# Projecting two head pairs per matmul, in a fused attention and expert layer on one core

## The chip, the cores and the metric

The kernel runs on one core of a Trainium2 chip. A core has a matrix engine (TensorE, PE in the profile; PEld are its weight loads), a vector engine (VectorE, DVE), an activation engine (ScalarE, ACT), a general engine (GpSimd, POOL) and a queue engine that starts transfers (SP). Each runs its own instructions in order, and they meet at semaphores only. TensorE writes its results to PSUM, which VectorE and ScalarE read. The metric is device time in microseconds (us): 525.79 us for the kernel before, the median of three runs (525.74 to 526.81).

## The reference

Input x is 16 rows of 256 tokens by 128 channels. The output is x plus two branches, both fed with the layer norm xn of x.

```
qkv = xn @ Wqkv + bqkv                       # 16 heads of 8
q, k = features(q), features(k)              # 8 -> 64: normalise, project with omega, clip, exp
out_t = sum_{s<=t} (q_t.k_s) v_s / max(sum_{s<=t} q_t.k_s, 1e-6)     # causal, no softmax
attention = out @ Wout + bout
logits = rms(xn) @ rms(slot_embeds)^T        # 256 tokens x 512 slots
slots = softmax(logits, tokens)^T @ rms(xn)
experts = softmax(logits, slots) @ (gelu(slots @ w1) @ w2)
```

## The kernel before, in words

One input row (256 tokens) is one turn of `row(b, ...)`; there are 16. Each engine has its own `row`, written out by hand as eight steps s = 0 to 7, one for each pair of heads. The order in it is the order of the engine's work, and every dependency is a semaphore wait (`after`, or `hold`, which waits in an instruction of its own). `bp` is the row before, `b1` the next, `b2` the one after that. So work of three rows is interleaved.

The attention of a row goes through these steps:

- `qkv_bias`, `qk_norms`, `qk_newton` (VectorE), `squares` and `qk_apply` (GpSimd) give normalised q and k of the next row. `stack_high` (ScalarE) and `stack_low` (GpSimd) write them as high and low fp16 parts into `stack`; `turn_stack` (SP queue) turns the stack round with one transposing transfer into `stack_t`.
- `project(b, p)` multiplies one pair's part of `stack_t` (96 rows) by omega, into the one PSUM bank `p_feat`: two matmuls of 256 columns, one for q and one for k. `clip` (VectorE) takes it to `arg`, `feature_exp` (ScalarE) to `feat`.
- `scores(b, p)` is eight matmuls with 64 rows and 64 columns of the array, four for each head of the pair, to the banks `p_sa` and `p_sb`. `evac_a` (VectorE, with the causal mask) and `evac_b` (ScalarE, masked after it by GpSimd's `mask_b`) take them to `s_sb`, which has four buffers.
- `context(b, a)` multiplies the scores of four heads (two pairs) by v into `p_ctx`, `ctx_copy` and `ctx_transposed` bring it to tokens by channels, `ctx_norm` divides. `attn_back`, `attn_copy`, `attention_out` are the output projection.

The experts of the same row are `logits`, `token_maxima` and `slot_maxima` (VectorE), `shift` (subtracts the maxima by matmuls, once `mx_ok` is up), the exponentials, `slot_sums`, `slots_transposed`, `hidden` in two halves, `gelu`, `processed`, `combine`. In TensorE's `row`, `project(b1, 0)` stands behind `hidden(b, nxt, 0)` at step 6, `project(b1, 1)` at the end of step 7, and `processed(bp)` before `scores(b, 0)`.

Of the kernel before, what the change touches and what calls it, by code (L numbers as in the profile page):

```python
# [16 lines left out]
PAIRS = HEADS // 2  # L17
# [44 lines left out]
def v_col(a):  # L62

    return (HD + 1) * (a % 3)
# [20 lines left out]
def build(nc, x, Wqkv, bqkv, Wout, bout, omega, nodes, weights, gamma_x, gamma_slot, slot_embeds,  # L85
          w1, w2, out):
    with ExitStack() as ctx:
# [34 lines left out]
        node_b = sb("node_b", [32, R])  # L122
        node_b2 = sb("node_b2", [32, R])
        om_scale = sb("om_scale", [32, R])
# [6 lines left out]
        omega_f = sb("omega_f", [32, PAIRS, 128])  # L131
        omega_st = sb("omega_st", [96, PAIRS, 128], F16)
# [14 lines left out]
        stack = sb("stack", [128, 2, 4, TILES, 4, 32], F16)  # L147
        stack_t = sb("stack_t", [128, 2, 2, 4, T], F16)
        vw = sb("vw", [128, 2, TILES, HEADS, 32])
        feat = sb("feat", [128, 4, 2 * T])  # L150
        arg = sb("arg", [128, 2, 2 * T])
        s_sb = sb("s_sb", [128, 4, 2, 384])
# [19 lines left out]
        p_feat = pb("p_feat", [128, 512])  # L172
        p_sa = pb("p_sa", [128, 512])
        p_sb = pb("p_sb", [128, 512])
        p_ctx = pb("p_ctx", [128, 2, T])
# [56 lines left out]
        ft_ok = sem("ft_ok")  # L232
        cl_ok = sem("cl_ok")
# [39 lines left out]
        def stacked(a):  # L273
            return stack[:, :, :, :, a, :].rearrange("p k g j d -> p j (k g) d")

        def parted():
            return qk_n[:, :, :].rearrange("p j (h d) -> p j h d", d=32)
# [5 lines left out]
        def _(sp):  # L283
# [13 lines left out]
            def turn_stack(b):  # L297
                hold(sp, sthi_ok, count(b, 1, 1))
                hold(sp, stlo_ok, count(b, 1, 1))
                hold(sp, ft_ok, count(b, 8, -8))  # L300
                sp.dma_start_transpose(stack_t[:, b[1], :, :, :].rearrange("p k g (j t) -> p (k g j) t", t=128),
                                       stack[:, :, :, :, :, :].rearrange("p k g j a d -> p (k g j a d)")
                                       ).then_inc(d_st, 16)
# [19 lines left out]
            for hl in range(4):  # L323
                for r in range(R):
                    src = omega[r].rearrange("(g q) d m -> q d g m", q=4)[hl]
                    dst = omega_f[8 * hl:8 * hl + 8, :, :].rearrange("d (g u) f -> d g u f", u=2)[
                        :, :, hl // 2, 64 * (hl % 2) + 32 * r:64 * (hl % 2) + 32 * r + 32]
                    sp.dma_start(dst, src).then_inc(d_om, 16)
# [29 lines left out]
        def _(pool):  # L358
            pool.memset(omega_f[:, :, :], 0.0).then_inc(om_zero, 1)
            pool.memset(stack[:, :, :, :, 3, :], 0.0).then_inc(st_zero, 1)  # L360
# [62 lines left out]
            def mask_b(b, p):  # L423
                hold(pool, eb_ok, count(b, 8, p + 1))
                v = s_sb[:, p % 4, 1, :].rearrange("p (a t) -> p a t", t=128)[:, 0:3:2, :]
                m = causal[:, :].rearrange("p (a t) -> p a t", t=128)[:, 0:3:2, :]
                pool.tensor_tensor(v, v, m, ALU.mult).then_inc(mb_ok, 1)  # L427
# [26 lines left out]
        def _(act):  # L454
# [26 lines left out]
            def feature_exp(b, p):  # L481
# [3 lines left out]
                nc.scalar.activation(feat[:, p % 4, :], arg[:, p % 2, :], ACT.Exp, bias=f_bias[:, 0:1]).then_inc(fe_ok, 1)  # L485

            def evac_b(b, p):
                after(act, sb_ok, count(b, 8, p + 1))
                after(act, cx_ok, count(b, 4, p // 2 - 1))
                nc.scalar.activation(s_sb[:, p % 4, 1, :], p_sb[:, 0:384], ACT.Copy).then_inc(eb_ok, 1)  # L490

            def ctx_copy(b, g):
                after(act, cx_ok, count(b, 4, 3 + g))
                after(act, ct_ok, count(b, 1, 0))
                nc.scalar.activation(ctx_sb[:, g, :], p_ctx[:, g, :], ACT.Copy).then_inc(cs_ok, 1)  # L495
# [18 lines left out]
            def gelu(b):  # L514
                for half, bank in enumerate((x01, x23)):
                    after(act, hd_ok, count(b, 2, half + 1))
                    nc.scalar.activation(hid_t[:, 2 * half:2 * half + 2, :], bank[:, :, :],  # L517
                                         ACT.Gelu).then_inc(ge_ok, 1)
# [10 lines left out]
            spread(bqkv_bc, bqkv, 3 * C).then_inc(d_rows, 16)  # L529

# [29 lines left out]
            def row(b, first, nxt, nxt2):  # L560

                b1, b2, bp = step(b, 1), step(b, 2), step(b, -1)
                for s in range(8):
                    if s == 0 and not first:
                        proc_copy(bp)
# [6 lines left out]
                    if s == 5:  # L572
                        combine_exp(b)
                    if s == 6:
                        slots_high(b)
                    if s == 7:
                        gelu(b)
                        if nxt:
                            nc.scalar.preload_act_table_set(LN_EXP)
                        ctx_copy(b, 0)  # L580
                        if nxt:
                            feature_exp(b1, 0)
                    if s == 0:
                        feature_exp(b, 1)
# [3 lines left out]
                    if s == 0:  # L588
                        if not first:
                            ctx_copy(bp, 1)  # L590
                        if nxt:
                            xt_high(b1)
                    if s == 4 and nxt:
                        stack_high(b1)
                    if s == 5 and nxt2:
                        ln_root(b2)

            run_rows(act, row)
            last_row = (B // 2 - 1, 1)
            proc_copy(last_row)  # L600
            ctx_copy(last_row, 1)
# [4 lines left out]
        def _(dve):  # L606
# [66 lines left out]
            def clip(b, p):  # L673

                after(dve, ft_ok, count(b, 8, p + 1))
                after(dve, fe_ok, count(b, 8, p - 1))
                nc.vector.tensor_scalar(arg[:, p % 2, :], p_feat[:, :], f_low[:, 0:1], f_high[:, 0:1], ALU.max,  # L677
                                        ALU.min).then_inc(cl_ok, 1)

            def evac_a(b, p):  # L680
                after(dve, sa_ok, count(b, 8, p + 1))
                after(dve, cx_ok, count(b, 4, p // 2 - 1))
                nc.vector.tensor_tensor(s_sb[:, p % 4, 0, :], p_sa[:, 0:384], causal[:, :], ALU.mult).then_inc(ea_ok, 1)  # L683

            def ctx_norm(b):
# [3 lines left out]
                for j in range(TILES):  # L689
                    last = nc.vector.tensor_scalar(  # L690
                        den[:, j, 0:12].rearrange("p (a q) -> p q a", q=QUADS),
                        t[:, 0, j, :, HD:HD + 19:9], DEN_FLOOR, None, ALU.max)
                nc.vector.tensor_scalar(den[:, :, 12:16], t[:, 1, :, :, HD], DEN_FLOOR, None,
                                        ALU.max).then_inc(dn_ok, 1)
# [4 lines left out]
                for a in range(4):  # L699
                    rows = t[:, a // 3, :, :, v_col(a):v_col(a) + HD]  # L700
# [72 lines left out]
            dve.wait_ge(d_om, 16 * 8)  # L773
            for r in range(R):
                v = omega_f[:, :, :].rearrange("p a (h r m) -> p (a h) r m", h=2, r=R)[:, :, r, :]
# [7 lines left out]
            nc.vector.tensor_copy(omega_st[0:32, :, :], omega_f[:, :, :])  # L783
            nc.vector.tensor_copy(omega_st[32:64, :, :], omega_f[:, :, :]).then_inc(om_s, 1)
            dve.wait_ge(om_s, 2)
            nc.vector.tensor_tensor(omega_st[64:96, :, :], omega_f[:, :, :], omega_st[0:32, :, :],
                                    ALU.subtract).then_inc(om_s, 1)
# [22 lines left out]
            clip(b0, 0)  # L810
            dve.wait_ge(se_h, 1)
# [8 lines left out]
            def row(b, first, nxt, nxt2):  # L820

                b1, b2, bp = step(b, 1), step(b, 2), step(b, -1)
                for s in range(8):
# [9 lines left out]
                    if s < 7:  # L833
                        clip(b, s + 1)
                    elif nxt:
                        clip(b1, 0)
                    if s == 5:
                        slots_norm(b)
                    if s == 2 and not first:
# [4 lines left out]
                    if s == 2 and not first:  # L844
                        add_attention(bp)
                    if s == 2 and nxt:
                        qk_norms(b1)
# [285 lines left out]
```

## Time and profile before

| | |
|---|---|
| Median of three runs | 525.79 us |
| Profiled execution | 526.66 us, of which the span from first to last instruction is 524.9 us |
| TensorE busy | 473.5 us, 90% |
| VectorE busy | 354.4 us, 68% |
| ScalarE busy | 319.9 us, 61% |
| GpSimd busy | 175.4 us, 33% |
| Granted TensorE clock over the span | 1.00 |

A row of input takes about 30 us on every engine, since the rows are interleaved. Busy matmuls overlap: a matmul's time in the trace holds its way through the array, and the next one starts before it ends. What a matmul costs TensorE is therefore read from start to start. The same holds, less strongly, for two operations of VectorE in a row.

### The profile page before, as it was taken

The numbers are of one execution on the slowest core, as the hardware profiler recorded it, in microseconds if no ns is written. First come the engines' busy times: TensorE is split into PE (matmuls) and PEld (weight loads), VectorE is DVE, ScalarE is ACT, GpSimd is POOL, SyncE is SP. The second block draws the span as 40 slices with busy tenths as digits, with TensorE's granted clock in tenths as the row PEclk, the third lists the DMA queues.
The fourth block names the chain that finished last, engine by engine and source line by source line (L and its number), as shares of the span: only waits on it lengthen the run. The fifth ranks groups of instructions, "written<-read, shape, count | busy, mean of one in ns | idle before, by whom it ended". The sixth has DMA issues, their size and how long they took to land.

```text
span 524.9 us, 15159 instructions
## 1 busy us (share of the span) xinstructions
PE 473.5 (90%) x5384; PEld 378.6 (72%) x5384; DVE 354.4 (68%) x905; ACT 319.9 (61%) x560; POOL 175.4 (33%) x278
## 2 busy tenths in 40 slices
PE   4049899999999999999999999999999999999996
PEld 2037686877878787787878687787768778787775
DVE  3667587585958768594966858595775859585561
ACT  3225747667573757658484766758476675847562
POOL 4314243251424334152424325141432514243220
PEclk9999999999999999999999999999999999999999
DMA  2220202020020202002020200102020110202000
GB/s 68 64 51 2 51 12 52 1 43 22 12 51 10 50 0 55 5 10 50 10 50 5 55 0 20 40 10 50 10 50 0 37 23 10 41 12 42 12 2 10
DMA packets 45362, 14.41 MB, mean 27 GB/s; under 512 B 35224, under 2 KB 45208, under 8 KB 45336
## 3 DMA queue, kind: packets, MB, share of 16 engines
q1 hardware_dynamic: 44904, 13.80, 12.6%
q8 instruction: 16, 0.26, 0.2%
q10 hardware_dynamic: 432, 0.26, 0.2%
q14 instruction: 10, 0.08, 0.0%
HBM read 3.57 MB, written 2.10 MB: 11 GB/s over the span
## 4 chain that ended last, share of the span: by engine, by line
PE 69%; DMA 14%; ACT 5%; POOL 4%; issue 4%; SPq 2%; DVE 1%; POOLq 0%; ACTq 0%; DVEq 0%
PE x L867 18%; DMA stack_t<-stack 13%; PE p_sa L903 12%; PE x L1016 11%; PE p_ctx L920 8%; PE x L1026 5%; PE p_feat L892 5%; POOL stack L421 3%; ACT stack L478 3%; PE x L945 2%; PE x L933 2%; PE x L972 2%; PE x L980 1%; PE p_sb L903 1%; ACT ctx_sb L495 1%
## 5 line engine op out<-in xcount | busy, mean ns | idle before, releaser
L427 POOL TENSOR_TENSOR s_sb<-s_sb,causal 128x256 f32<-128x256 f32 x128 | 93.5, 730 | 270.5 <-ACT s_sb L490 268.7
L677 DVE TENSOR_SCALAR arg<-p_feat,f_low,f_high 128x512 f32<-128x512 f32 x128 | 103.1, 806 | 29.8 <-PE p_feat L892 27.4
L683 DVE TENSOR_TENSOR s_sb<-p_sa,causal 128x384 f32<-128x384 f32 x128 | 70.3, 549 | 59.7 <-PE p_sa L903 59.6
L490 ACT ACTIVATE s_sb<-p_sb 128x384 f32<-128x384 f32 x128 | 62.5, 489 | 76.7 <-PE p_sb L903 76.3
L903 PE MATMUL p_sa<-feat 64*64 64x256 f32 (+3 forms) x1024 | 100.0, 312 | 7.1 <-ACT s_sb L490 3.7
L485 ACT ACTIVATE feat<-arg,f_bias 128x512 f32<-128x512 f32 x128 | 91.6, 716 | 21.1 <-DVE arg L677 21.1
L903 PEld LDWEIGHTS p_sa<-feat 64*64 64x64 f32 x1024 | 76.2, 134 | 34.6 <-issue 27.5
L903 PE MATMUL p_sb<-feat 64*64 64x256 f32 (+3 forms) x1024 | 100.0, 313 | 0.0
L903 PEld LDWEIGHTS p_sb<-feat 64*64 64x64 f32 x1024 | 76.9, 134 | 0.0
L892 PE MATMUL p_feat<-stack_t,omega_st 96*128 96x256 f16 x256 | 50.8, 280 | 23.4 <-DMA stack_t<-stack 23.0
L1016 PE MATMUL x<-w_sb,hid_t 128*128 128x128 f32 x512 | 59.8, 275 | 0.0
L1016 PEld LDWEIGHTS x<-w_sb,hid_t 128*128 128x128 f32 x512 | 58.5, 192 | 0.3
L920 PE MATMUL p_ctx<-s_sb,vw 128*32 128x256 f32 (+1 forms) x1024 | 54.9, 332 | 1.1 <-issue 1.1
L892 PEld LDWEIGHTS p_feat<-stack_t,omega_st 96*128 96x128 f16 x256 | 20.0, 99 | 42.0 <-issue 38.0
L517 ACT ACTIVATE hid_t<-x 128x1024 f32<-128x1024 f32 x32 | 32.8, 1024 | 16.3 <-PE x L867 16.1
L920 PEld LDWEIGHTS p_ctx<-s_sb,vw 128*32 128x32 f32 x1024 | 27.4, 109 | 17.0 <-issue 1.9
L1026 PE MATMUL x<-proc,comb_t 128*128 128x129 f32 x256 | 31.2, 274 | 0.0
L988 PE MATMUL x<-xg,disp 128*128 128x129 f32 x256 | 31.2, 275 | 0.0
L988 PEld LDWEIGHTS x<-xg,disp 128*128 128x128 f32 x256 | 29.8, 191 | 0.2
L1026 PEld LDWEIGHTS x<-proc,comb_t 128*128 128x128 f32 x256 | 29.9, 191 | 0.2
L867 PE MATMUL x<-slot_hi,w_hi 128*128 128x512 f32 x64 | 28.6, 447 | 0.0
L500 ACT ACTIVATE attn_t<-x 128x256 f32<-128x256 f32 x16 | 6.1, 384 | 36.9 <-PE x L939 36.9
(134 smaller groups left out, 849.7 us busy)
## 6 DMA issues: line engine op xcount, KB each, us to landing
xin<-in_L_attn_x_dram SPq DMA_DIRECT2D x32, 64.0 KB, 2.4
out_dram<-out_sb SPq DMA_DIRECT2D x32, 64.0 KB, 2.1
se_rows<-n_L_ffn_slot_embeds_dram SPq DMA_DIRECT2D x1, 256.0 KB, 5.9
w_f<-in_L_ffn_w_dram SPq DMA_DIRECT2D x1, 256.0 KB, 6.1
w_sb<-in_L_ffn_w_dram SPq DMA_DIRECT2D x1, 256.0 KB, 4.8
stack_t<-stack SPq DMA_TRANSPOSE x16, 4.3
bqkv_bc<-in_L_attn_bqkv_dram ACTq DMA_DIRECT2D x1, 192.0 KB, 5.1
wqkv_f<-in_L_attn_Wqkv_dram SPq DMA_DIRECT2D x1, 192.0 KB, 5.1
```

The lines of the kernel that those rows point to most:

```text
L427: pool.tensor_tensor(v, v, m, ALU.mult).then_inc(mb_ok, 1)
L485: nc.scalar.activation(feat[:, p % 4, :], arg[:, p % 2, :], ACT.Exp, bias=f_bias[:, 0:1]).then_inc(fe_ok, 1)
L490: nc.scalar.activation(s_sb[:, p % 4, 1, :], p_sb[:, 0:384], ACT.Copy).then_inc(eb_ok, 1)
L677: nc.vector.tensor_scalar(arg[:, p % 2, :], p_feat[:, :], f_low[:, 0:1], f_high[:, 0:1], ALU.max, ALU.min).then_inc(cl_ok, 1)
L683: nc.vector.tensor_tensor(s_sb[:, p % 4, 0, :], p_sa[:, 0:384], causal[:, :], ALU.mult).then_inc(ea_ok, 1)
L867: mm = nc.tensor.matmul(dst, a, w, start=start and i == 0, stop=stop and i == 2, skip_group_check=True)
L892: mm = nc.tensor.matmul(p_feat[:, T * k:T * k + T], omega_st[:, p, :], stack_t[0:96, b[1], k, g, :], start=True, stop=True)
L903: mm = nc.tensor.matmul(bank[rows:rows + 64, o:o + hi - lo], f[:, T + keys:T + keys + 64], f[:, lo:hi], start=True, stop=True, skip_group_ ...
L920: mm = nc.tensor.matmul(p_ctx[32 * q:32 * q + 32, a // 3, 128 * kt:T], vw[:, b[1], kt, QUADS * a + q, :], s_sb[:, p % 4, q % 2, T * kt:T * ...
L988: mm = nc.tensor.matmul(x01[:, c // 2, 129 * (c % 2):129 * (c % 2) + 129], disp[:, j, 128 * c:128 * c + 128], xg[:, b[1], j, :], start=(j ...
L1016: mm = nc.tensor.matmul(x01[:, 1, 128 * c:128 * c + 128], hid_t[:, m, 128 * c:128 * c + 128], w2_sb[:, m, :], start=(m == 0 and c == 0), s ...
L1026: mm = nc.tensor.matmul(x23[:, 0, 129 * j:129 * j + 129], comb_t[:, c, 128 * j:128 * j + 128], proc[:, c, :], start=(c == 0), stop=(c == N ...
```

## The change

The projection now takes two pairs at once. `stack` is laid out in blocks of 64 rows for each pair (high, low, high, zero; 16 values each), so that after the transposition the two pairs of a group lie in rows 0 to 63 and 64 to 127. `project(b, g)` issues two matmuls of 512 columns, one for each half of the array's rows, into the banks `p_f` and `p_g`. There are four groups in a row of input instead of eight pairs. `omega` is loaded twice, half of its 16 transfers by ScalarE's queue. `arg` has four buffers.

To make room for the second bank, `p_ctx` is gone. The context goes into columns 384 to 511 of the two score banks, now one tensor `p_s`, in two lumps: contexts 0 and 1 at step 4, contexts 2 and 3 at step 0 of the next row between the two halves of `processed`. Since the scores now wait there for up to four pairs, `s_sb` has eight buffers. Context 0 and 2 wait until both engines that read the score banks are through with them, and scores 0 and 5 wait for `ctx_copy`.

The order of several steps changes with it: clips come up to two pairs earlier, `gelu` is cut in halves with `evac_b` of pair 7 between them, and `project(b1, 0)` stands ahead of `hidden`. The core of the diff:

```diff
-            def project(b, p):
+            def project(b, g):
                 after(pe, d_st, count(b, 16, 16))
-                after(pe, cl_ok, count(b, 8, p))
-                g = p // 2
-                for k in range(2):
-                    mm = nc.tensor.matmul(p_feat[:, T * k:T * k + T], omega_st[:, p, :],
-                                          stack_t[0:96, b[1], k, g, :], start=True, stop=True)
-                mm.then_inc(ft_ok, 1)
+                hold(pe, cl_ok, count(b, 8, 2 * g))
+                for u, (bank, done) in enumerate(((p_f, ft_ok), (p_g, fg_ok))):
+                    rows = slice(64 * u, 64 * u + 64)
+                    nc.tensor.matmul(bank[:, :], omega_st[rows, g, :],
+                                     stack_t[rows, b[1], :, :, g, :].rearrange("p j k t -> p k j t"), start=True,
+                                     stop=True).then_inc(done, 1)
...
             def scores(b, p):
+                if p in (0, 5):
+                    hold(pe, cs_ok, count(b, 2, p // 5))
...
             def context(b, a):
-                after(pe, ea_ok, count(b, 8, 2 * a + 2))
+                if a % 2 == 0:
+                    scored = (5, 8)[a // 2]
+                    after(pe, ea_ok, count(b, 8, scored))
+                    after(pe, eb_ok, count(b, 8, scored))
+                    after(pe, v_ok, count(b, 1, 1))
+                    after(pe, cs_ok, count(b, 2, a // 2))
...
-                for kt in range(TILES):
+                for kt, j in ((0, 0), (0, 1), (1, 1)):
                     for q in range(QUADS):
...
+                        mm = nc.tensor.matmul(p_s[32 * q:32 * q + 32, j, 384:512], vw[:, b[1], kt, QUADS * a + q, :],
...
@@ TensorE's row
                     if s == 0 and not first:
-                        processed(bp)
+                        processed(bp, 0)
+                        context(bp, 2)
+                        context(bp, 3)
+                        processed(bp, 1)
                     scores(b, s)
                     if s == 0:
                         if not first:
-                            context(bp, 3)
+                            ctx_transposed(bp)
                         if nxt:
                             transposes(b1)
-                        if not first:
-                            ctx_transposed(bp)
+                        project(b, 1)
...
                     if s == 6:
-                        context(b, 2)
-                        hidden(b, nxt, 0)
                         if nxt:
                             project(b1, 0)
+                        hidden(b, nxt, 0)
@@ VectorE's row
-                    if s < 7:
-                        clip(b, s + 1)
-                    elif nxt:
-                        clip(b1, 0)
+                    if s == 1:
+                        clip(b, 3)
+                    if s == 3:
+                        clip(b, 5)
                     if s == 5:
+                        clip(b, 7)
                         slots_norm(b)
+                    if s == 7 and nxt:
+                        clip(b1, 1)
...
                     evac_a(b, s)
...
+                    if s in (0, 2, 4):
+                        clip(b, s + 2)
+                    if s == 6 and nxt:
+                        clip(b1, 0)
                     if s == 2 and nxt:
                         qk_norms(b1)
```

The order of TensorE before, from the last matmuls of `scores(b, 6)` on (`p_ctx` is the context, `slot_hi` with `w_hi` are the first products of `hidden`, `p_feat` the projection of the next row):

```order
L903 MATMUL p_sa<-feat 64x128
L903 MATMUL p_sb<-feat 64x128
L920 MATMUL p_ctx<-s_sb,vw 32x256 x4
L920 MATMUL p_ctx<-s_sb,vw 32x128 x4
L867 MATMUL x<-slot_hi,w_hi 128x512
L867 MATMUL x<-slot_lo,w_hi 128x512
L867 MATMUL x<-slot_hi,w_lo 128x512
L867 MATMUL x<-slot_hi,w_hi 128x512
L867 MATMUL x<-slot_lo,w_hi 128x512
L867 MATMUL x<-slot_hi,w_lo 128x512
L892 MATMUL p_feat<-stack_t,omega_st 128x256 x2
```

And in the changed kernel, from the same place (`p_f` and `p_g` are the two banks of the projection):

```order
L925 MATMUL p_s<-feat 64x128 x2
L912 MATMUL p_f<-stack_t,omega_st 128x512
L912 MATMUL p_g<-stack_t,omega_st 128x512
L887 MATMUL x<-slot_hi,w_hi 128x512
L887 MATMUL x<-slot_lo,w_hi 128x512
L887 MATMUL x<-slot_hi,w_lo 128x512
L887 MATMUL x<-slot_hi,w_hi 128x512
L887 MATMUL x<-slot_lo,w_hi 128x512
L887 MATMUL x<-slot_hi,w_lo 128x512
```

The context of pairs 4 and 5 and the first half of `hidden` no longer stand between the scores and the projection of the next row; the projection comes right behind the scores.

The order of VectorE before, from the last projection that it clips ahead of the maxima (`arg<-p_feat` is a clip, `out_sb` is `add_attention`, the reduce to `small` is `qk_norms`, `maxima` the two kinds of maxima):

```order
L677 TENSOR_SCALAR arg<-p_feat,f_low,f_high 128x512
L737 RECIPROCAL comb_rs<-x 128x2
L741 SCALAR_TENSOR_TENSOR ffn_res<-x,comb_rs,xres 128x128 x2
L683 TENSOR_TENSOR s_sb<-p_sa,causal 128x384
L749 TENSOR_TENSOR out_sb<-x,ffn_res 128x256
L662 TENSOR_REDUCE small<-qk_sq 128x64
L665 TENSOR_SCALAR small<-small 128x64
L710 TENSOR_REDUCE maxima<-x 128x2
L716 TENSOR_REDUCE maxima<-x 128x2 x2
L677 TENSOR_SCALAR arg<-p_feat,f_low,f_high 128x512
```

And in the changed kernel, from `add_experts` on:

```order
L747 RECIPROCAL comb_rs<-x 128x2 [waits fi_ok]
L751 SCALAR_TENSOR_TENSOR ffn_res<-x,comb_rs,xres 128x128 [waits xr_ok,rf_ok]
L751 SCALAR_TENSOR_TENSOR ffn_res<-x,comb_rs,xres 128x128
L694 TENSOR_TENSOR s_sb<-p_s,causal 128x384 [waits cx_ok,sa_ok]
L759 TENSOR_TENSOR out_sb<-x,ffn_res 128x256 [waits o1_ok,wo_ok]
L688 TENSOR_SCALAR arg<-p_f,f_low,f_high 128x512 [waits fe_ok,ft_ok]
L672 TENSOR_REDUCE small<-qk_sq 128x64 [waits sq_ok]
L675 TENSOR_SCALAR small<-small 128x64 [waits red_ok]
L720 TENSOR_REDUCE maxima<-x 128x2 [waits lg_ok]
L726 TENSOR_REDUCE maxima<-x 128x2 [waits lg_ok] x2
```

The clip of pair 4, which stood behind the maxima, stands ahead of `qk_norms` and of the maxima.

The start of the same stretch in the changed kernel, from `evac_a(b, 0)` on (`xt_lo` belongs to the next row, `den`, `rden` and `attn` are `ctx_norm`):

```order
L694 TENSOR_TENSOR s_sb<-p_s,causal 128x384 [waits cx_ok,sa_ok]
L688 TENSOR_SCALAR arg<-p_f,f_low,f_high 128x512 [waits fe_ok,ft_ok]
L657 TENSOR_TENSOR xt_lo<-x,xt_hi 128x256 [waits xth_ok]
L688 TENSOR_SCALAR arg<-p_g,f_low,f_high 128x512 [waits fe_ok,fg_ok]
L694 TENSOR_TENSOR s_sb<-p_s,causal 128x384 [waits cx_ok,sa_ok]
L701 TENSOR_SCALAR den<-x 128x2x4x2 [waits ct_ok]
```

The clip of pair 2 comes before `xt_lo`; before the change `xt_lo` came first, and the clip of pair 3 stood behind `ctx_norm` and `qkv_bias`.

## Rows read from the trace of the kernel before

**Rows 1.** Chain that ended last: starts (us) and lengths of the stack's transfer.

```profile
84.25 4.68 DMA stack_t<-stack
...
447.05 4.29 DMA stack_t<-stack
```

**Rows 2.** Busy time by engine in three stretches that make one row.

```profile
240.35:247.07 6.72, 6.50 (x58) 5.55 (x59) 2.56 (x6) 5.49 (x8) 0.14 (x1) 1.00 0.03 10
247.07:259.61 12.54, 12.40 (x146) 10.31 (x150) 10.27 (x26) 5.46 (x13) 5.23 (x10) 1.00 0.04 10
259.61:270.32 10.71, 10.04 (x141) 7.40 (x130) 8.57 (x25) 8.52 (x16) 5.15 (x6) 1.00 0.27 52
```

**Rows 3.** Timeline of TensorE: start, length, what, and idle time before it.

```profile
240.35 0.39 PE L892 MATMUL p_feat<-stack_t,omega_st 96*128 96x256 f16 x2 [0.41 <-DMA stack_t<-stack]
240.67 0.43 PE L903 MATMUL p_sa<-feat 64*64 64x256 f32 x1
...
241.37 0.50 PE L867 MATMUL x<-slot_hi,w_hi 128*128 128x512 f32 x1
...
242.88 0.39 PE L892 MATMUL p_feat<-stack_t,omega_st 96*128 96x256 f16 x2
243.11 3.74 PE L1016 MATMUL x<-w_sb,hid_t 128*128 128x128 f32 x32
247.07 0.40 PE L903 MATMUL p_sa<-feat 64*64 64x256 f32 x1 [0.22 <-ACT s_sb L490]
...
247.78 0.86 PE L920 MATMUL p_ctx<-s_sb,vw 128*32 128x256 f32 x16
248.56 0.44 PE L875 MATMUL x<-ident,xg 128*128 128x128 f32 x2
249.14 0.66 PE L933 MATMUL x<-ident,ctx_sb 128*128 128x128 f32 x4
...
261.22 0.41 PE L903 MATMUL p_sa<-feat 64*64 64x256 f32 x1
```

**Rows 4.** Timeline of VectorE over steps 1 to 3 of the same row.

```profile
249.46 0.42 DVE L647 TENSOR_TENSOR xt_lo<-x,xt_hi 128x256 fp32r<-128x256 f32 x1 [0.92 <-ACT xt_hi L467]
250.05 0.81 DVE L677 TENSOR_SCALAR arg<-p_feat,f_low,f_high 128x512 f32<-128x512 f32 x1 [0.17 <-PE p_feat L892]
...
251.24 0.25 DVE L690 TENSOR_SCALAR den<-x 128x12 f32<-128x12 f32 x2
...
253.56 0.80 DVE L677 TENSOR_SCALAR arg<-p_feat,f_low,f_high 128x512 f32<-128x512 f32 x1
254.28 0.16 DVE L737 RECIPROCAL comb_rs<-x 128x2 f32<-128x2 f32 x1
...
256.03 0.68 DVE L662 TENSOR_REDUCE small<-qk_sq 128x64 f32<-128x512 f32 x1
...
257.19 1.23 DVE L710 TENSOR_REDUCE maxima<-x 128x2 bf16<-128x1024 f32 x1
258.33 1.28 DVE L716 TENSOR_REDUCE maxima<-x 128x2 bf16<-128x512 f32 x2
259.52 0.80 DVE L677 TENSOR_SCALAR arg<-p_feat,f_low,f_high 128x512 f32<-128x512 f32 x1
260.24 0.55 DVE L683 TENSOR_TENSOR s_sb<-p_sa,causal 128x384 f32<-128x384 f32 x1
```

**Rows 5.** Timeline of GpSimd: normalising q and k of the next row.

```profile
261.58 1.08 POOL L413 TENSOR_TENSOR qk_n<-qkv,small 128x512 f32<-128x512 f32 x1 [0.84 <-DVE small L614]
```

**Rows 6.** The chain that ended last, from there to the transfer.

```profile
263.16 1.15 ACT stack L478 x2
...
264.57 1.16 POOL stack L421
...
265.92 4.26 DMA stack_t<-stack
```

**Rows 7.** Timeline of ScalarE: taking the scores of pair 4.

```profile
262.16 0.49 ACT L490 ACTIVATE s_sb<-p_sb 128x384 f32<-128x384 f32 x1 [0.17 <-PE p_sb L903]
```

## What the change was predicted to do

> **What bounds the kernel now.** I read the shares of busy time first: TensorE is at 90%, VectorE at 68%. That would say that halving the projections pays. But the chain that ended last goes, in every row, through the transfer of the stack, so the question is what TensorE would do if it had less work. The starts of that transfer give the period: (447.05 - 84.25) / 12 rows = 30.23 us a row [rows 1]. Then I took one row apart at three places where engines meet:
>
> - stretch 1, from `project(b1, 0)` to `scores` of pair 0: 6.72 us, of which TensorE is busy 6.50;
> - stretch 2, from there until the maxima are done (VectorE's 258.33 + 1.28 = 259.61 us): 12.54 us, TensorE 12.40, VectorE 10.27;
> - stretch 3, from the maxima to the next `project(b1, 0)`: 10.71 us, with three engines and the transfer in it one after another [rows 2].
>
> Together that row is 29.97 us. The reader is to see two near ties. TensorE arrives at `project(b1, 0)` 0.41 us before the stack has landed [rows 3]: it and the chain to the stack run neck and neck. And VectorE, from its clip at 250.05 us on, has work without a gap up to the maxima [rows 4], which are done 0.4 us before TensorE gets to `shift`. Two chains beside TensorE are thus as long as TensorE's own work. A change that takes work from TensorE gains only where both get shorter too; one that moves work of TensorE out from beside them loses.
>
> **Stretch 3, maxima to `project(b1, 0)`.** Nothing in the chain goes away: clip, `evac_a`, `qk_newton` on VectorE, `qk_apply` on GpSimd, `stack_high` on ScalarE, `stack_low` on GpSimd, the transfer. From the maxima to the start of `qk_apply` it is 261.58 - 259.61 = 1.97 us, `qk_apply` takes 1.08 [rows 5]. Before, `stack_high` came 0.50 us later, since ScalarE still had the scores of pair 4 to take. That falls to about 0.1: without context 0 ahead of `shift`, pair 4 is scored earlier against the maxima. Then 264.57 - 263.16 = 1.41 to `stack_low`, 1.35 to the transfer, 4.26 for it and 0.13 to TensorE [rows 6]. The sum is 1.97 + 1.08 + 0.1 + 1.41 + 1.35 + 4.26 + 0.13 = 10.30; I take 10.35, against 10.71. The layout has the same number of values, so the transfer and the copies keep their cost; runs are 16 values long, not 32, for which no row has a price. I bound that by 0.3 us either way, about the spread of 4.26 to 4.68 in the transfer's own rows [rows 1, 6].
>
> TensorE needs less than that. Context 2 (0.78 us, 247.78 to 248.56) and the first half of `hidden` (242.88 - 241.37 = 1.51) no longer stand ahead of the projection; context 0 comes in (0.78), and with it a new wait: it writes in the banks of the scores, so it waits until pair 4 has been taken, 262.16 + 0.49 - 261.22 = 1.43 us after that pair's scores began, while scores and projection end after 0.95 [rows 3, 7]. That costs 0.5 us. TensorE arrives 1.0 us earlier than now, and adds this to the 0.4 that it waits already, less the 0.36 of the shorter chain: it waits about 1.1 us for the stack. The new wait is hidden under that, and so is the saved projection. Behind the waiting `project(b1, 0)` stand both halves of `hidden`, `scores` 7 and `processed`, all of which used to begin before it or right behind it.
>
> The Trainium skill (PSUM — Partial Sum Buffer, section on PSUM bank collisions) says that TensorE and a reader must be kept apart by bank and group of 32 partitions, whatever the columns. That the spare columns are free does not make the bank free, and the wait of 0.5 us can't be dropped. No row of this trace shows the bank shared.
>
> **Stretch 1, `project(b1, 0)` to `scores` of pair 0.** All of it is TensorE's own work, so it adds up [rows 3]: projection 0.25, `hidden` 1.51, `scores` 0.70 (240.67 to 241.37), `hidden` 1.51, `processed` 3.74 (243.11 to 247.07 less its wait of 0.22), and now contexts 2 and 3. Sum without contexts 7.71. A context takes 0.78 us now; it keeps its 4 x 384 columns but has 12 matmuls for 8. If only columns count, two are 1.56; if each matmul costs what it does now (0.78 / 8), 2.34. I take 1.6, since in `processed` matmuls of 128 columns follow each other every 3.74 / 32 = 0.117 us without a gap. 7.71 + 1.6 = 9.3; I take 9.2, the second projection (0.23) and the 0.22 wait being gone already. That is 2.5 us more than 6.72. Most of it was work done beside the stack's chain before. `gelu` and the exponentials are covered: `gelu`'s first half has the scores and the second half of `hidden` (2.2 us) ahead of its reader, the second half has 3.4 us.
>
> **Stretch 2, `scores` of pair 0 to the maxima.** TensorE loses context 3 (0.78), its wait for `ctx_copy` and one projection of three (0.23): 12.40 - 0.78 - 0.23 = 11.4 us [rows 2, 3]. VectorE does not lose. Its chain now starts at the clip of pair 2, which waits for the projection behind the transposes: 0.71 for the scores, about 0.27 and 0.49 for the transposes (0.44 and 0.66 less the 0.16 by which a matmul's time overlaps the next), 0.39 + 0.04 for the projection = 1.90. Then, start to start [rows 4]: clip 0.72, `xt_low` 0.35, clip 0.72, `evac_a` 0.47, `ctx_norm` and `qkv_bias` 253.56 - 251.24 = 2.32, `add_experts`, `evac_a` and `add_attention` 256.03 - 254.28 = 1.75, clip 0.72, `qk_norms` 1.16, token maxima 1.14, slot maxima 1.28. That is 10.63, and 12.5 with the start, as long as now (12.54). Two edits cancel: the chain starts 1.1 us earlier against the scores, and takes in `xt_low` and the clip of pair 4, which stood behind the maxima. TensorE waits about 1.1 us at `shift`, where it waited for nothing.
>
> Here the Trainium skill speaks against the change (TensorEngine Tiling (Array Packing), sections on the PSUM bottleneck and on tiling modes): packing speeds up TensorE but not the emptying of PSUM, which may become the bound, and a change of tiling mode drains the array. By the first, stretch 2 is VectorE's, as the sum above has it. By the second, the projection, now alone in its mode, pays a switch on both sides. A row with a switch shows its size: `hidden` after `scores` starts with 0.50 us instead of about 0.40 [rows 3]. At 0.1 us for two projections on the path this adds 0.2 us a row, within my range.
>
> **Sum.** 10.35 + 9.2 + 12.5 = 32.05 us a row, 1.8 more than 30.23. It counts in the 14 rows that have a row before and one behind: 25.5 us. The first and last rows: the first has no `ctx_norm` and no `add_experts`, so TensorE's saving shows in its stretch 2, and the loss of stretch 1 follows; the last has no stack to wait for. I take +1 for both, between -2 and +3. The doubled loads of omega and ScalarE's queue end before the first stack is written; nothing. 526.66 + 26.5 = 553.2 for a profiled execution, which lay 0.9 above the median of the runs: 552.3, say **552 us**.
>
> **Rivals.**
>
> 1. *Only the stack counts.* VectorE's operations follow each other more closely than start to start in the old order, or TensorE's matmuls are slower, so that `shift` does not wait. Stretch 2 is then 11.4, a row 30.95, and the time 526 + 14 x 0.7 + 1 = 537 us. For it: VectorE's chain holds small waits of its own. Against: it has no gap in rows 4.
> 2. *The halves don't run side by side*, or the contexts cost by the matmul. Two projections on the path at 0.43 instead of 0.22 and 0.7 for the contexts: +1.1 us a row at most, 560 to 567 us. This is also the case in which the change doesn't do what it says. Against: `scores` already uses row halves with two banks, four matmuls in the time of one.
> 3. *Faster: TensorE bounds throughout.* The place is `project(b1, 0)`; it decides whether the stack lands before TensorE has scored pair 6. If the chain to it is shorter by the 1.1 us of the wait, and the maxima come as in rival 1, a row is 32.05 - 1.1 - 1.1 = 29.85, and the time 526 - 14 x 0.4 = 520 us. For it: TensorE is busy 90%, and four projections fewer are 0.9 us. Against: TensorE waits for the stack even now, behind 2.3 us of work that goes away from there.
>
> **How the numbers follow.** Forecast 0.62, rival 1 0.20, rival 2 0.08, rival 3 0.07, no change 0.03 (gain and loss cancel). The forecast's own range is 545 to 559: half a microsecond a row either way. The range 534 to 560 takes in rival 1 and leaves out rival 3 and the top of rival 2. This kernel's timings tell a difference from about 0.2% on, 1 us (three of them lie within that). Faster 0.07, same 0.03, slower 0.90.
>
> **What would show it.** Right: TensorE idles about 1 us in every row at the projection into `p_f`, released by the stack's transfer; it idles about 1 us at `shift`, released by the slot maxima; stretches of about 9.2, 12.5 and 10.35 us; a context of four heads takes about 0.8 us. Wrong: no idle time at one of the two (rival 1 or 3), a projection of 512 columns that takes 0.43 us start to start, or a transfer much shorter than 4.26 us.

## The result, and the profile after

The changed kernel takes 575.68 us (median of four runs, 573.13 to 578.53) against 525.84 us: a ratio of 1.0945, 95% interval 1.0877 to 1.1013. It is slower, as forecast, but 9.5% and not 5%, and it lies outside the stated range of 534 to 560 us. Its profiled execution took 578.53 us, with a span of 576.5 us. Of all executions below, one, of the version v1, took 671.46 us at a granted clock of 0.673 and is left out of v1's figures.

The page of the changed kernel shows first what is new. In part 2 each digit is a slice of 14.4 us, and PEclk is TensorE's granted clock in tenths:

```profile
PE 484.0 (84%) x5768; PEld 394.3 (68%) x5768; DVE 348.8 (61%) x889; ACT 322.6 (56%) x560; POOL 174.1 (30%) x278
...
PEclk9999899979999799999989899898999989998999
...
L912 PE MATMUL p_f<-stack_t,omega_st 64*128 64x512 f16 x64 | 25.7, 402 | 41.4 <-DMA stack_t<-stack 41.4
```

TensorE idles 41.4 us ahead of the projection, where it was 23.0 before (some 18 us of both is the first row's start). And its clock is no longer full: the mean granted clock is 0.961, where it was 1.000. At a mean of 0.961 between 1.2 and 2.4 GHz, 7.8% of the span, or 45 us, ran at half speed. That is a measure of time and not yet of loss: six executions of the kernel before are on record at a mean of 0.970 to 0.971 and took 525.55 to 527.02 us, hardly more than those at 0.998 to 1.000 (524.72 to 526.99 us). What counts is where the half clock falls.

I cut two rows as in [rows 2], from `project(b1, 0)` to `scores` of pair 0, to the maxima, to the next `project(b1, 0)`. The first three lines are a row in which the clock stayed full, the next three one in which it did not, and the last line is the first stretch of a third row, the longest of all (columns as in [rows 2]; the last but two is the granted clock):

```profile
225.99:235.42 9.43, 9.43 (x110) 7.84 (x111) 3.36 (x10) 6.50 (x8) 0.77 (x2) 1.00 0.03 8
235.42:247.82 12.40, 11.32 (x121) 9.48 (x120) 10.62 (x26) 4.94 (x11) 4.65 (x9) 1.00 0.04 11
247.82:258.58 10.76, 7.79 (x130) 6.29 (x131) 7.12 (x20) 8.59 (x17) 5.11 (x6) 1.00 0.28 55
...
326.47:337.42 10.95, 10.95 (x110) 8.84 (x111) 3.45 (x10) 6.37 (x8) 0.73 (x1) 0.84 0.01 4
337.42:349.73 12.31, 11.31 (x121) 9.48 (x120) 10.58 (x26) 4.87 (x11) 4.66 (x9) 1.00 0.04 11
349.73:360.29 10.56, 7.79 (x131) 6.32 (x132) 7.13 (x20) 8.39 (x17) 5.10 (x6) 1.00 0.28 55
...
190.92:203.14 12.22, 12.22 (x111) 9.67 (x111) 3.44 (x10) 6.41 (x8) 0.73 (x1) 0.74 0.02 4
```

The two whole rows differ most in the stretch right behind the wait for the stack: 9.43 us at full clock, 10.95 at 0.84. Cut in the same way, this stretch takes 9.42 or 9.43 us at a clock of 1.00 in five of the 15 rows, and 10.91 to 12.22 us at 0.74 to 0.84 in the other ten. Together the ten are 18.6 us longer than ten of 9.43 us. The timeline of TensorE around that wait answers to [rows 3]:

```profile
324.05 0.77 PE L925 MATMUL p_s<-feat 64*64 64x256 f32 x16 [0.39 <-ACT feat L491]
326.47 0.37 PE L912 MATMUL p_f<-stack_t,omega_st 64*128 64x512 f16 x1 [1.65 <-DMA stack_t<-stack]
326.47 0.39 PE L912 MATMUL p_g<-stack_t,omega_st 64*128 64x512 f16 x1
326.79 0.67 PE L887 MATMUL x<-slot_hi,w_hi 128*128 128x512 f32 x1
327.25 0.63 PE L887 MATMUL x<-slot_lo,w_hi 128*128 128x512 f32 x1
...
330.95 0.39 PE L887 MATMUL x<-slot_lo,w_hi 128*128 128x512 f32 x1
331.18 0.40 PE L887 MATMUL x<-slot_hi,w_lo 128*128 128x512 f32 x1
...
332.12 1.95 PE L1040 MATMUL x<-w_sb,hid_t 128*128 128x128 f32 x16
333.99 1.52 PE L943 MATMUL p_s<-s_sb,vw 128*32 128x128 f32 x48
335.44 2.05 PE L1040 MATMUL x<-w_sb,hid_t 128*128 128x128 f32 x16
337.42 0.78 PE L925 MATMUL p_s<-feat 64*64 64x256 f32 x16
```

The two row halves of the projection start at the same time and are followed 0.32 us later. The reader is to see the same form of matmul, 128 rows by 512 columns, take 0.63 us and follow each other every 0.43 us behind the wait, and 0.39 and 0.23 us from 330.95 on. The windows around it give the clock:

```profile
323.50:326.50 3.00, 0.97 (x20) 0.69 (x18) 1.16 (x2) 2.76 (x7) 1.39 (x2) 1.00 0.89 175
326.50:330.40 3.90, 3.90 (x18) 2.57 (x22) 2.89 (x9) 1.58 (x2) 0.00 (x0) 0.56 0.04 10
330.40:334.30 3.90, 3.90 (x46) 3.44 (x42) 0.56 (x1) 2.71 (x4) 0.73 (x1) 1.00 0.00 0
```

TensorE was busy 0.97 of 3.00 us, and then did 3.9 us of work at 0.56 of its clock. Six microseconds cut behind each of the 15 later stack transfers show a clock of 0.51 to 0.72 in ten and 1.00 in five. TensorE had waited 1.42 to 2.18 us for the stack ahead of the ten and 1.33 to 1.64 us ahead of the five, so the length of the wait alone does not tell the two kinds apart. The rule in the Trainium skill (TensorE: Matmul & The Clock Gate, the part on the clock gate) that an array left idle falls back to half its clock and has to work to get it back agrees with the ten rows; the five show that a wait of this length does not always bring it about.

The other waits of the row, still from TensorE's timeline:

```profile
340.63 0.44 PE L887 MATMUL x<-wqkv_hi,xt_hi 128*128 128x384 f32 x1 [0.60 <-DVE xt_lo L657]
...
349.79 0.62 PE L996 MATMUL x<-neg_ident,maxima 128*128 128x128 bf16 x8 [0.45 <-DVE maxima L726]
...
352.54 1.52 PE L943 MATMUL p_s<-s_sb,vw 128*32 128x128 f32 x48 [0.43 <-DVE s_sb L694]
353.99 2.05 PE L1012 MATMUL x<-xg,disp 128*128 128x129 f32 x16
...
357.04 0.66 PE L1021 MATMUL x<-ident,slot_v 128*128 128x128 f32 x4 [0.30 <-DVE slot_v L736]
```

Contexts 0 and 1 take 353.99 - 352.54 = 1.45 us here, as long as 2 and 3 above (333.99 to 335.44).

### The profile page after: what moved, and what is told of

Read it like the earlier page. It is cut to its first block, busy times and chain, and to the rows that moved or that the text cites. A ratio compares the mean times of both kernels' runs of the same rounds, so it can differ in the third digit from the quotient of the medians.

```text
span 576.5 us, 16010 instructions
## 1 busy us (share of the span) xinstructions
PE 484.0 (84%) x5768; PEld 394.3 (68%) x5768; DVE 348.8 (61%) x889; ACT 322.6 (56%) x560; POOL 174.1 (30%) x278
## 4 chain that ended last, share of the span: by engine, by line
PE 53%; DMA 13%; DVE 13%; issue 9%; ACT 4%; POOL 4%; SPq 2%; DVEq 1%; POOLq 0%; ACTq 0%
PE x L887 15%; DMA stack_t<-stack 12%; PE x L1040 10%; PE p_s L925 9%; PE x L1051 5%; PE p_s L943 4%; DVE arg L688 4%; POOL stack L427 3%; DVE maxima L720 3%; PE p_f L912 2%; ACT stack L484 2%; DVE maxima L726 2%; PE x L966 2%; DVE small L672 2%; PE x L954 2%
## 5 line engine op out<-in xcount | busy, mean ns | idle before, releaser
L694 DVE TENSOR_TENSOR s_sb<-p_s,causal 128x384 f32<-128x384 f32 x128 | 70.6, 552 | 122.9 <-PE p_s L925 122.5
L925 PE MATMUL p_s<-feat 64*64 64x256 f32 (+3 forms) x2048 | 104.7, 322 | 10.3 <-ACT feat L491 6.2
L925 PEld LDWEIGHTS p_s<-feat 64*64 64x64 f32 x2048 | 82.8, 139 | 42.8 <-issue 33.4
L496 ACT ACTIVATE s_sb<-p_s 128x384 f32<-128x384 f32 x128 | 62.8, 490 | 85.2 <-PE p_s L925 84.9
L688 DVE TENSOR_SCALAR arg<-p_f,f_low,f_high 128x512 f32<-128x512 f32 x64 | 51.6, 806 | 26.1 <-PE p_f L912 26.1
L912 PE MATMUL p_f<-stack_t,omega_st 64*128 64x512 f16 x64 | 25.7, 402 | 41.4 <-DMA stack_t<-stack 41.4
L943 PE MATMUL p_s<-s_sb,vw 128*32 128x128 f32 x1536 | 48.6, 274 | 6.7 <-DVE s_sb L694 6.7
L688 DVE TENSOR_SCALAR arg<-p_g,f_low,f_high 128x512 f32<-128x512 f32 x64 | 51.3, 801 | 0.0
L943 PEld LDWEIGHTS p_s<-s_sb,vw 128*32 128x32 f32 x1536 | 40.2, 110 | 13.1 <-DVE s_sb L694 11.2
L1051 PEld LDWEIGHTS x<-proc,comb_t 128*128 128x128 f32 x256 | 30.7, 191 | 0.6 <-ACT proc L528 0.5
L887 PE MATMUL x<-slot_hi,w_lo 128*128 128x512 f32 x64 | 30.4, 476 | 0.0
L887 PE MATMUL x<-slot_lo,w_hi 128*128 128x512 f32 x64 | 30.3, 473 | 0.0
```

Source lines behind the costliest of these rows:

```text
L496: nc.scalar.activation(s_sb[:, p, 1, :], p_s[:, 1, 0:384], ACT.Copy).then_inc(eb_ok, 1)
L688: nc.vector.tensor_scalar(arg[:, p % 4, :], bank[:, :], f_low[:, 0:1], f_high[:, 0:1], ALU.max, ALU.min).then_inc(cl_ok, 1)
L694: nc.vector.tensor_tensor(s_sb[:, p, 0, :], p_s[:, 0, 0:384], causal[:, :], ALU.mult).then_inc(ea_ok, 1)
L887: mm = nc.tensor.matmul(dst, a, w, start=start and i == 0, stop=stop and i == 2, skip_group_check=True)
L912: nc.tensor.matmul(bank[:, :], omega_st[rows, g, :], stack_t[rows, b[1], :, :, g, :].rearrange("p j k t -> p k j t"), start=True, stop=Tru ...
L925: mm = nc.tensor.matmul(p_s[rows:rows + 64, u, o:o + hi - lo], f[:, T + keys:T + keys + 64], f[:, lo:hi], start=True, stop=True, skip_grou ...
```

## The experiments

Each ratio is to executions of the kernel before on the same chip, whose medians lie between 525.34 and 525.68 us.

**fill: the wait stays, the idle time goes.** Two matmuls whose results are overwritten fill most of the wait for the stack.

```diff
+            def fill(b):
+                hold(pe, cl_ok, count(b, 8, 8))
+                w = w2_sb[:, :, :].rearrange("p m c -> p (m c)")
+                for n in (512, 256):
+                    nc.tensor.matmul(p_f[:, 0:n], ident[:, :], w[:, 0:n], start=True, stop=True)
...
                         if nxt:
+                            fill(b)
                             project(b1, 0)
```

> The changed kernel with two extra fp32 matmuls (512 and 256 columns, about 1.28 us, results overwritten) into p_f right ahead of project(b1, 0), where TensorE idles 1.4 to 1.65 us for the stack. They add work and take no wait away. Theory A (the idle makes the clock drop to 0.50 for about 3.4 us in 10 of 15 rows, and that costs 17 to 22 us): the granted clock goes to 0.99 or more, no half-speed stretch follows the projection, and the time falls by 15 to 22 us, to 554 to 561 us. Rival B (the clock drops for another reason, such as the projection's half-array tiles or the idle at shift): clock stays near 0.96 and the time stays at 573 to 579 us. Rival C (the extra work costs by itself): slower than 576.

Measured: 558.63 us (557.87 to 559.26), ratio to the kernel before 1.0631 (1.0602 to 1.0660), granted clock 1.000. A kernel with two matmuls more in each of 15 rows is 17 us faster. Its windows for the same three stretches:

```profile
315.51:324.96 9.45, 9.43 (x110) 7.87 (x110) 3.36 (x10) 6.41 (x8) 0.74 (x1) 1.00 0.02 7
324.96:337.27 12.31, 11.32 (x121) 9.48 (x120) 10.58 (x26) 4.87 (x11) 4.66 (x9) 1.00 0.04 11
337.27:347.82 10.55, 9.20 (x134) 6.96 (x134) 7.13 (x20) 8.38 (x17) 5.07 (x6) 1.00 0.29 56
```

They equal those of the changed kernel's full-clock row within 0.1 us in the first two and 0.2 in the third; TensorE's busy time in the last rose from 7.79 to 9.20. So 17 of the 50 us were clock (14 to 21 by single executions, and 18.6 by the ten stretches above), lost because TensorE stood idle, and rival B (another cause of the drop) falls.

**fill_half.** Only the 512-column matmul, so that part of the idle time stays.

```diff
-                for n in (512, 256):
+                for n in (512,):
```

> The kernel of fill with only the 512-column matmul (0.85 us), so that 0.5 to 0.8 us of the idle time at project(b1, 0) stays. If a short idle does no harm (idles of 0.3 to 0.6 us did none in the traces of before and hidden_first): clock 0.99 or more and 554 to 560 us. If any idle there can drop the clock: clock between 0.96 and 0.99 and 560 to 573 us.

Measured: 558.18 us (558.08 to 558.78), ratio 1.0612 (1.0594 to 1.0630), clock 0.999. What is left of the wait ahead of the projection, 0.23 to 1.09 us in 14 rows, does no harm here; the clock was 1.00 also behind the longest. The first line is that one, the second a usual one:

```profile
154.15 0.37 PE L912 MATMUL p_f<-stack_t,omega_st 64*128 64x512 f16 x1 [1.09 <-DMA stack_t<-stack]
...
348.47 0.37 PE L912 MATMUL p_f<-stack_t,omega_st 64*128 64x512 f16 x1 [0.36 <-DMA stack_t<-stack]
```

**before_early: the order alone, in the kernel before.** Nothing of the new projection, banks or buffers.

```diff
                     if s == 6:
-                        context(b, 2)
-                        hidden(b, nxt, 0)
                         if nxt:
                             project(b1, 0)
+                        context(b, 2)
+                        hidden(b, nxt, 0)
```

> The kernel before with one edit: project(b1, 0) right behind scores(6), ahead of context 2 and the first half of hidden. Projection, banks and buffers are those of before. Theory A: TensorE idles about 2.6 us there in 15 rows; the row grows by 2.3 us less what later waits give back, and the clock drops after the idle. Without clock loss 526 + 15 x 2.2 = 559; with 1.2 to 1.7 us a row of clock loss 577 to 585 us. Rival B (the loss belongs to the new projection and the shared banks): under 535 us. Rival D (wait but no clock loss): 555 to 562 at a granted clock of 1.00.

Measured: 583.55 us (582.17 to 585.82), ratio 1.1111 (1.1070 to 1.1153), clock 0.930. One call in another place costs the kernel before 11%, more than the whole change. TensorE waits 2.68 us:

```profile
331.57 0.39 PE L892 MATMUL p_feat<-stack_t,omega_st 96*128 96x256 f16 x2 [2.68 <-DMA stack_t<-stack]
...
332.67 0.65 PE L867 MATMUL x<-slot_hi,w_hi 128*128 128x512 f32 x1
333.12 0.63 PE L867 MATMUL x<-slot_lo,w_hi 128*128 128x512 f32 x1
```

It waits 2.36 to 3.35 us in the 15 rows, and the 9 us behind the wait show a clock of 0.72 to 0.81 in 14 of them and 1.00 in one. The mean of 0.930 holds something else as well. From 12.2 to 42.6 us, ahead of and behind the first transfer of the stack, this execution ran at half clock, where the profile of the kernel before shows 1.00:

```profile
12.20:30.80 18.60, 0.00 (x0) 0.00 (x1) 11.53 (x36) 4.69 (x18) 5.55 (x8) 0.50 0.36 85
30.80:42.60 11.80, 10.24 (x71) 7.16 (x72) 7.83 (x13) 3.98 (x8) 2.50 (x3) 0.50 0.00 1
```

These 30 us cost nothing that the rows show: the stack's second transfer starts at 53.11 us, at 53.85 in the kernel before and at 53.20 in `before_early_fill` below.

**before_early_fill.** The same with about 2.1 us of overwritten matmuls in that wait.

```diff
+            def fill(b):
+                hold(pe, ec_ok, count(b, 1, 1))
+                w = w2_sb[:, :, :].rearrange("p m c -> p (m c)")
+                for n in (512, 512, 256):
+                    nc.tensor.matmul(x23[:, 0, 0:n], ident[:, :], w[:, 0:n], start=True, stop=True)
```

> before_early (the kernel before with project(b1, 0) right behind scores(6)) with three fp32 matmuls of 512, 512 and 256 columns (about 2.1 us, results overwritten, in a bank that hidden writes next) ahead of that projection, where TensorE idles 2.68 us. Theory A (about 1.6 us of each row's loss is clock, about 2.2 us the wait itself): clock 0.99 or more, row 32.4 to 32.6 us, time 556 to 563 us. Rival (the clock drop costs nothing, since later waits take it up): 580 to 586 us, as before_early.

Measured: 561.32 us (561.23 to 561.42), ratio 1.0672 (1.0654 to 1.0689), clock 1.000. Here too the clock part can be taken away by itself: 22 us of 58. The other 36 us are the wait and what follows from it.

**hidden_first: the cover put back, in the changed kernel.**

```diff
                     if s == 6:
+                        hidden(b, nxt, 0)
                         if nxt:
                             project(b1, 0)
-                        hidden(b, nxt, 0)
```

> The changed kernel with the first half of hidden ahead of project(b1, 0) again; all else as changed. Theory A (the misplaced cover is the loss, first as a wait and then as clock): the wait for the stack goes, hidden waits about 0.45 us for slots_low instead, no clock drop. Row: 12.3 (scores 0 to maxima) + 11.1 (maxima to the projection, now TensorE's own work and waits) + 7.7 = 31.1 us, time 526.7 + 14 x 0.87 + 1 = about 540 us, between 535 and 545. Rival B (VectorE's chain to the maxima or the shared score banks are the main loss): 555 us or more.

Measured: 548.91 us (548.26 to 549.18), ratio 1.0440 (1.0414 to 1.0467), clock 1.000. The wait for the stack and the clock loss are gone, 27 us together; the time is 9 us above what I expected. The row is 31.8 us on average (32.00 in the one shown) and not 31.1, since other waits follow:

```profile
341.70 0.50 PE L887 MATMUL x<-slot_hi,w_hi 128*128 128x512 f32 x1 [0.68 <-DVE slot_lo L741]
...
348.07 1.52 PE L943 MATMUL p_s<-s_sb,vw 128*32 128x128 f32 x48 [0.31 <-DVE s_sb L694]
```

`hidden` waits for the low part of the slots, since context 2 no longer stands ahead of it (I had put 0.45 us on that), and context 2 for `evac_a` of pair 7, which I hadn't seen.

**v1: four places reordered.** To `hidden_first` it adds:

```diff
-                        context(b, 0)
-                        context(b, 1)
                         slot_sums(b, 0)
+                        context(b, 0)
+                        context(b, 1)
                         slot_sums(b, 1)
...
-                        if not first:
-                            ctx_transposed(bp)
                         if nxt:
                             transposes(b1)
+                        if not first:
+                            ctx_transposed(bp)
...
-                    if s == 1 and nxt:
-                        xt_low(b1)
+                    if s == 0 and nxt:
+                        xt_low(b1)
                     if s in (0, 2, 4):
                         clip(b, s + 2)
```

> The changed kernel with four places reordered: hidden's first half ahead of project(b1, 0); slot_sums(0) ahead of contexts 0 and 1, as cover for their wait on the score banks; the transposes of the next row ahead of ctx_transposed; xt_low ahead of the clip of pair 2 on VectorE. Theory A: the waits of 1.5 (stack), 0.43 (banks) and 0.60 (qkv_product on xt_low) go, VectorE's chain shortens by 0.35; row 29.8 to 30.2 us, time 518 to 526 us, clock 1.00. Rival (another engine's chain takes each wait's place): 535 us or more.

Measured: 537.96 us (537.72 to 538.21, three executions), ratio 1.0234 (1.0201 to 1.0266), clock 0.999. The time falls by 11 us and not to the expected 518 to 526 us; it lies where the rival had it, at 535 us or more. The waits for the banks and at `qkv_product` are gone, but TensorE now waits longer for the maxima (0.63 us, where it was 0.44 in `hidden_first`), and the wait of `hidden` stays:

```profile
325.41 0.62 PE L996 MATMUL x<-neg_ident,maxima 128*128 128x128 bf16 x8 [0.63 <-DVE maxima L726]
326.64 0.77 PE L925 MATMUL p_s<-feat 64*64 64x256 f32 x16 [0.17 <-issue]
...
334.86 0.50 PE L887 MATMUL x<-slot_hi,w_hi 128*128 128x512 f32 x1 [0.68 <-DVE slot_lo L741]
```

**v2.** Three more places, of which the first was a mistake:

```diff
                     if s == 3:
                         token_maxima(b)
                         slot_maxima(b)
+                        if nxt:
+                            qk_norms(b1)
...
-                    if s == 2 and nxt:
-                        qk_norms(b1)
...
+                    if s == 5:
+                        feature_exp(b, 6)
                     evac_b(b, s)
```

(Not shown: `evac_a` of pair 7 ahead of the next row's clip 1, and `qk_root` moved to step 4, besides.)

> v1 with three more places reordered: the maxima ahead of qk_norms on VectorE (qk_root on ScalarE moved behind the exponential of pair 4 with it), evac_a of pair 7 ahead of the clip of the next row's pair 1, and the exponential of pair 6 ahead of evac_b of pair 5. Theory A: of v1's waits of TensorE in a row, 0.63 (shift) falls to 0.3, 0.31 (context 2) goes, 0.39 (scores 6) falls to at most 0.2; row 31.15 - 0.8 = 30.35, at worst 30.6; time 525 to 531 us. Rival B (the stack lands late again, as its chain now has qk_norms in it): a wait of 0.3 us or more at project(b1, 0) and 531 to 537 us.

Measured: 548.05 us (546.87 to 548.87), ratio 1.0421 (1.0397 to 1.0444), clock 0.993. Slower than v1, by neither theory's path: `qk_norms` has joined the clip ahead of `evac_a` of pair 3, for which pair 4's scores wait. They wait 1.36 us in every row; in two of the 15 the clock then drops to half, as in the row shown, and in the others it stays full:

```profile
333.23 0.97 PE L927 MATMUL p_s<-feat 64*64 64x256 f32 x16 [1.36 <-DVE s_sb L696]
```

**v3.** v1 with v2's other two edits, and the clip of pair 4 behind the maxima as in the kernel before:

```diff
                     if s == 3:
-                        clip(b, 5)
+                        clip(b, 4)
...
                     evac_a(b, s)
...
-                    if s in (0, 2, 4):
+                    if s in (0, 4):
                         clip(b, s + 2)
+                    if s == 3:
+                        clip(b, 5)
```

> v1 with three edits: the clip of pair 4 right behind the maxima instead of ahead of qk_norms; evac_a of pair 7 ahead of the clip of the next row's pair 1; the exponential of pair 6 ahead of evac_b of pair 5. Theory A: the maxima come 0.72 us earlier, so shift doesn't wait, and scores(4) waits for its exponential instead (0.4 us less in sum); context 2's wait of 0.31 goes, and 0.43 us between slots_transposed and hidden. Row 31.15 - 1.1 to 1.2 = 30.0 us, time 521 to 526 us. Rival B (the stack's transfer, which v1 had 0.8 us ahead of its reader, becomes late): waits of over 0.3 us at project(b1, 0), 526 to 532 us. Rival C (each wait removed comes back elsewhere): 535 us or more.

Measured: 539.14 us (537.35 to 540.18, five runs), ratio 1.0257 (1.0239 to 1.0275), clock 1.000. No gain over v1, and rival C holds: the wait at the maxima fell to 0.37 us, and 0.50 came at the scores behind it. Rival B's waits came too, in the first rows: `project(b1, 0)` waits for the stack 1.61, 1.02 and 0.90 us in three rows (all at full clock), and less later. Row by row, by the starts of the transfer, v3 takes 32.37, 31.49 and 31.46 us there and then 30.7, against 31.03 in v1's mean; a gain of 0.3 us in each later row is lost in the first ones.

```profile
325.33 0.62 PE L1000 MATMUL x<-neg_ident,maxima 128*128 128x128 bf16 x8 [0.37 <-DVE maxima L728]
325.79 0.60 PE L1008 MATMUL x<-neg_ident,maxima 128*128 128x256 bf16 x4
326.89 0.77 PE L929 MATMUL p_s<-feat 64*64 64x256 f32 x16 [0.50 <-ACT feat L491]
```

No version with the new projection beat the kernel before.

## Why the prediction was wrong, step by step

**The sign and the place were right.** TensorE waits for the stack at `project(b1, 0)` in every row, and `hidden` and context 2 are the cover that it lost. `hidden_first` takes that wait away and `before_early` makes it by itself.

**The step that failed is the sum.** It takes stretch 1 at 9.2 us, since "All of it is TensorE's own work, so it adds up", from rows at a granted clock of 1.00, for a TensorE that it had just made idle for over 1 us. In ten rows of fifteen the clock fell to half behind that wait, and the stretch took 10.91 to 12.22 us. No term and no rival had the clock. `fill` measures the missing term: 575.7 - 558.6 = 17 us. Without it the kernel lies at 558.6 us, against the forecast of 552 and inside the range. Most of the other 6.6 us are in the row: by the starts of the stack's transfer a row of `fill` takes 32.42 us on average, 2.2 more than the 30.23 of the kernel before, where the sum had 1.8. The sum was built from a row of 29.97 us and then set against the mean of 30.23.

**The sizes of the rest**, at full clock:

| | forecast | changed, full clock | fill |
|---|---|---|---|
| `project(b1, 0)` to `scores` 0 | 9.2 | 9.43 | 9.45 |
| `scores` 0 to the maxima | 12.5 | 12.40 | 12.31 |
| maxima to `project(b1, 0)` | 10.35 | 10.76 | 10.55 |
| row | 32.05 | 32.59 | 32.31 |

- Stretch 1: contexts cost 1.45 us for two, where columns alone gave 1.56 and the number of matmuls 2.34, so the columns count; rival 2 falls, the halves of the projection run side by side. In the full-clock row the terms are 0.32 for the projection, 1.60 and 1.50 for the halves of `hidden`, 0.71 for the scores, 1.87 and 1.98 for those of `processed` and 1.45 for the contexts, 9.43 in all. The prediction had 1.51 for each half of `hidden`, 3.74 for `processed` and 0.25 for the projection; for this last, the row that it read from already shows 0.32 (240.35 to 240.67 in [rows 3]). It also took off 0.1 us for a projection and a wait that its sum of 9.3 did not hold. That steps cost more behind a change of tile shape is in line with the rule on tiling modes in the Trainium skill (TensorEngine Tiling (Array Packing)) that the prediction had weighed and left in the range; no run isolates it.
- Stretch 2: VectorE's chain was right within 0.2 us. TensorE's 1.1 us of waiting came out in sum, but that is luck in part: 0.45 of it is at `shift`, where the prediction had put all, and 0.60 at `qkv_product`, which it did not have. Rival 1 falls.
- Stretch 3: 0.2 to 0.4 us longer than summed; the wait for the stack was 1.33 to 2.18 us and not 1.1. Rival 3 falls.

**Where the expected saving of the projection went.** Four projections fewer are 0.9 us of TensorE by [rows 3]. In one full-clock row TensorE's busy time went from 28.94 us [rows 2, sum of the three] to 9.43 + 11.32 + 7.79 = 28.54: 0.4 us. Of the missing 0.5 us, about 0.36 is the new projection's own cost (four times 0.32 us, against the 0.23 counted for one pair) and 0.11 `processed` cut in two (3.85 us for 3.74); other small terms were not measured one by one. And no order that I tried takes what is left: `hidden_first` and v1 have next to no wait for the stack and are still 4.4% and 2.3% slower than the kernel before, through waits of 0.3 to 0.7 us for VectorE and ScalarE, the longest of them (`shift`, `hidden`) at places where the old order had a context as cover. Of the 50 us, by the runs in order, 17 are clock, 10 the cover of the stack at full clock (`fill` to `hidden_first`), 11 the three waits of v1, and 12 are not undone by any order that I tried. The split depends on the order in which the edits are taken, and which part of the last 12 us belongs to the shared banks and which to order stays open.

## What to carry to other kernels

Before moving a step ahead of others on the busiest engine, ask what those others covered: here two pieces of 0.8 and 1.5 us stood in the shadow of a transfer, and bringing them out cost more than the whole edit could save. Where a sum makes TensorE idle for over a microsecond, price what follows at half clock as well, as a rival with a chance of its own; a fill of overwritten matmuls tells the two losses apart in one run. A mean clock over the whole execution does not price the loss; the length of the same stretch at either clock does. And when two chains on other engines are as long as the busiest engine's work, look for what shortens those chains first: here fewer matmuls alone saved nothing in any order tried.

## What the runs showed of the hardware

- Waits of TensorE of 1.33 to 2.18 us, once a row, were followed by half its granted clock in ten rows of 15 (changed kernel), waits of 2.36 to 3.35 us in 14 of 15 (`before_early`), and waits of 1.36 us in two of 15 (v2). Single waits of 1.09 us (`fill_half`) and 1.61 us (v3) left it at 1.00, and so did waits of 0.2 to 0.7 us, several in a row of v1 (0.999 over the whole). What decides in the range between is not shown.
- The 18 us at the start of the kernel in which TensorE waits for the first stack left the clock at 1.00 in the profile of the kernel before, and at 0.50, up to 42.6 us, in that of `before_early`.
- A drop cost 1.5 to 2.8 us in the stretch of 9.43 us behind it (changed kernel).
- Matmuls with 64 rows and 128 columns of the array, one in each row half and each to its own bank, start within 0.01 us of each other, and 512 columns of both are followed after 0.32 us.
- Twelve matmuls of 128 columns in four column groups took 0.73 us (half of the 1.45 for two contexts), where eight of 256 and 128 columns took 0.78 [rows 3].
